# A graph network on Trainium2: residual, norm and tables of the last layer as one stage by blocks

## The chip, the cores and the metric

One core of a Trainium2 chip runs the whole kernel as one program. The metric is the time on the device in microseconds (us), lower is better. A measurement of this kernel scatters by some 0.1% (6551.42 to 6558.74 us in three runs).

## The reference

A graph of 6250 nodes with 128 features each and 100,000 edges goes through two blocks, each with a residual:

```python
h = jnp.maximum(_layernorm(x, axis=-1), 0.0)
x = x + _L0_gnn_ref(h, edge_index, ...)
h = jnp.maximum(_layernorm(x, axis=-1), 0.0)
x = x + _L1_gnn_ref(h, edge_index, ...)
```

The first block, `_L0_gnn_ref`, is two layers of graph attention with three heads (GATv2). Each is followed by a dense layer over the nodes and a batch norm (mean and variance of each feature over all nodes) with a Relu:

```python
x_in = _gatv2(x, edge_index, Wl1, bl1, Wr1, br1, att1, bc1)
h = jax.nn.relu(_batchnorm(x_in @ W1 + b1, g1, be1))
h2 = _gatv2(h, edge_index, Wl2, bl2, Wr2, br2, att2, bc2)
out = jnp.concatenate([h2, x_in], axis=1) @ W2 + b2
return jax.nn.relu(_batchnorm(out, g2, be2))
```

The second block, `_L1_gnn_ref`, makes a query from one end of each edge and a key and a value from the other (`embeds @ qTrans`, `kTrans`, `vTrans`), weighs the values by a clipped exponential per head, sums them for each node, adds `embeds`, and ends with a layer norm that has a scale and a bias:

```python
out = (res - mu) * jax.lax.rsqrt(var + 1e-06) * ln_scale + ln_bias
```

## The kernel before

The nodes are padded to 49 blocks of 128. An array of all nodes by 128 features is one tile of 128 x 6272 float32 (49 blocks side by side). `k.y2` and `k.hT` are two such tiles. `k.hT`, and `k.y2` up to the residual, hold a feature in each partition (a column is a node). From the residual on `k.y2` holds a node in each partition (a block's 128 columns are its features). Both lie in the tile `feat_area`, with a work area behind them; `node_area` holds other arrays by node.

The program is a series of stages. Each is a `nc.Block()`: every engine runs its own function, semaphores inside it set the order of the work, and a stage begins on every engine only when all engines have ended the one before it. `k.recycle()` is a small stage of its own in which SyncE clears, one after the other, all semaphores that were taken since the last recycle. `pipeline(...)` writes a loop over the blocks, unrolled by two, in which every engine goes round a ring of two buffers.

The stages that matter here, in order:

- **First layer's end.** `batch_norm` (tag "1", L1702) finds scale and shift of the batch norm from `k.hT`. `relu_in_place` (L1758) applies them and the Relu to all of `k.hT` by one ScalarE instruction (L1765). `k.recycle()` follows.
- **Tables of the second GATv2 layer.** `node_tables`, by `table_parts` (L1105): for each block ScalarE takes the features into a stage buffer (`take`, L1167), TensorE multiplies them by two weight matrices (L1157, L1158), ScalarE copies one product to a buffer (`copy`, L1173) from which SyncE stores it to DRAM (L1143), and VectorE keeps the other in SBUF. Take and copy go round two buffers each, and a copy waits until the store from its buffer has landed.
- **The edges, the dense layer** and `batch_norm` (tag "2") on `k.y2`.
- **Residual**, `residual_rows` (L1772): SyncE loads x (3.2 MB) into the place of `k.hT` (L1008, L1010); VectorE waits for all of it. For each block ScalarE applies scale, shift and Relu (L1788), TensorE turns the block so that a partition is a node (L1799), and VectorE adds x to it and writes it back to `k.y2` (L1811). Then `k.recycle()`.
- **Norm**, `norm_to_features` (L1095) by `norm_parts` (L1038) and `center` (L1013): VectorE and ScalarE go over the whole 128 x 6272 array one instruction at a time (sum L1018, subtract the mean L1020, square L1052, sum L1022, scale L1030); then for each block Relu on ScalarE (L1060), a transpose on TensorE (L1069) and a copy on VectorE into `k.hT` (L1083); at the end VectorE applies the Relu to the rows (L1086).
- **Tables of the attention**, `node_tables` again with other weights: key and value together (256 columns, L1157) go to DRAM, the query (128 columns, L1158) stays (`keep`, L1197).
- **Edges of the attention**, `edge_attention`; its first row on SyncE's queue is L1863.
- **The end**, `finish` (L1985): VectorE divides (L2036 to L2038), adds the features (L2041), takes mean and variance of each block (`bn_stats` L2043, `bn_aggr` L2046), ScalarE scales each block (L2027), VectorE multiplies by `ln_scale` and adds the residual (L2058, L2059) and SyncE stores. Beside this GpSimd adds `ln_bias` to the whole residual `k.y2` by one instruction (L2019).

## Time and profile before

| | |
|---|---|
| Time, median of 3 runs | 6554.96 us (6551.42 to 6558.74) |
| The profiled execution's own time | 6546.25 us, 8.71 us below that median |
| Its span, first to last instruction | 6544.4 us |
| Busy: PE, DVE, ACT, POOL | 76%, 85%, 66%, 61% of the span |
| Mean granted TensorE clock | 0.91 of 2.4 GHz |
| Residual to the last table, 5193.05 to 5367.15 us | 174.10 us |
| First layer's Relu, L1765 | 5.61 us |
| The end, from 6476.2 us | 68 us |

PE is TensorE, DVE VectorE, ACT ScalarE, POOL GpSimd, SP SyncE; a q behind a name is the engine's sequencer, which issues its instructions and DMAs. A clock of 1.00 is 2.4 GHz, of 0.50 it is 1.2 GHz. Where stages follow each other with a barrier, the time of the whole is the sum of the stages, and within a stage the loop's slowest chain sets the time, not the busiest engine's share. The idle time in brackets behind a row of the timeline is that of the row's engine before it, with what ended it.

### The profile page before, as it was taken

The page shows a single profiled execution, that of the slowest core. Times are in us where ns is not written, and L with a number is a line of the kernel's source. Part 1 is how long each engine was busy: PE and PEld are TensorE (multiplying, and loading weights), DVE is VectorE, ACT ScalarE, POOL GpSimd, SP SyncE. Part 2 cuts the span into 40 slices and gives each one's busy share as a digit, 9 for nine tenths or more (in the row PEclk, how much of TensorE's full clock was granted, in tenths as well). Part 3 has the DMA queues.
Part 4 walks back from the last instruction along what each step waited for, and adds up shares of the span by engine and source line. Part 5 has one row for each costly group of instructions (what it writes and reads, how often), then busy time and mean ns, then how long its engine had stood idle before and what let it go on. Part 6 is the DMA issues. An engine that isn't in the chain of part 4 may idle for free. (4 is left out here: it accounts for less than half of the span.)

```text
span 6544.4 us, 130007 instructions
## 1 busy us (share of the span) xinstructions
PE 4986.5 (76%) x23046; PEld 2906.8 (44%) x23047; DVE 5557.6 (85%) x13086; ACT 4324.9 (66%) x19265; POOL 3959.7 (61%) x3547
## 2 busy tenths in 40 slices
PE   3796899842888889888878899889998645555663
PEld 2573455421444444444463444444444435555552
DVE  9999988732999999999857999999999547777777
ACT  5576799720899999999837999999999430000001
POOL 0588877785666666666405666666665017777774
PEclk9999999966999999999989999999999767777776
DMA  0362000132555555555515555555556024444444
GB/s 13 62 81 22 2 2 2 11 53 52 146 139 139 140 139 139 140 139 140 100 41 144 140 140 140 139 141 141 139 139 128 23 67 127 127 126 126 126 126 73
DMA packets 397652, 656.25 MB, mean 100 GB/s; under 512 B 141767, under 2 KB 259461, under 8 KB 397044
## 3 DMA queue, kind: packets, MB, share of 16 engines
q0 software_dynamic: 185888, 481.62, 29.0%
q1 hardware_dynamic: 211540, 172.59, 11.3%
q14 instruction: 199, 1.63, 0.1%
q8 instruction: 25, 0.41, 0.0%
HBM read 617.73 MB, written 33.88 MB: 100 GB/s over the span
## 5 line engine op out<-in xcount | busy, mean ns | idle before, releaser
L1272 POOL DMA_INDIRECT feat_area<-xl_table,feat_area x1856 | 2007.0, 1081 | 1476.7 <-PE bank L1346 668.4
L1423 ACT ACTIVATE feat_area<-feat_area 128x130 f32<-128x130 f32 x5568 | 1643.5, 297 | 237.2 <-DVE feat_area L1476 234.0
L1333 PE MATMUL bank<-node_area,feat_area 128*128 x3712 | 1472.3, 520 | 339.4 <-DVE feat_area L1468 174.4
L1407 ACT ACTIVATE feat_area<-feat_area 128x128 f32<-128x128 f32 x4640 | 1442.1, 387 | 30.7 <-issue 30.7
L1346 PE MATMUL bank<-feat_area 128*128 128x390 f32 x3712 | 1408.9, 502 | 33.7 <-ACT feat_area L1407 12.6
L634 POOL DMA_INDIRECT rec_by_dst<-feat_area,gather_col x800 | 1051.2, 1314 | 243.7 <-issue 233.1
L1856 POOL DMA_INDIRECT feat_area<-kv_table,feat_area x832 | 829.4, 997 | 562.3 <-DMA feat_area<-gather_src 309.0
L1333 PEld LDWEIGHTS bank<-node_area,feat_area 128*128 128x128 f32 x3712 | 634.7, 190 | 988.8 <-issue 731.1
L1423 ACT ACTIVATION_READ_ACCUMULATOR feat_area<-feat_area 128x1 f32 x5568 | 1040.2, 187 | 0.0
L1346 PEld LDWEIGHTS bank<-feat_area 128*128 128x128 f32 x3712 | 670.2, 190 | 601.6 <-issue 196.0
L1468 DVE TENSOR_TENSOR feat_area<-bank,feat_area 128x780 f32<-128x780 f32 x928 | 889.6, 959 | 24.4 <-DMA feat_area<-xl_table,feat_area 17.8
L1476 DVE SCALAR_TENSOR_TENSOR feat_area<-feat_area 128x780 f32<-128x780 f32 x928 | 889.6, 959 | 0.0
L1911 ACT ACTIVATE feat_area<-feat_area 128x32 f32<-128x32 f32 x208 | 47.7, 230 | 1052.7 <-DVE feat_area L1952 1052.7
L1898 PE MATMUL bank<-feat_area 128*128 128x136 f32 x1664 | 357.6, 378 | 448.3 <-DVE feat_area L1963 448.1
L835 PE MATMUL bank<-feat_area 125*128 125x416 f16 x3200 | 571.4, 340 | 8.5 <-ACT feat_area L856 8.5
L856 ACT ACTIVATE feat_area<-feat_area 125x128 f16<-125x128 f16 x1600 | 514.2, 391 | 70.4 <-DVE feat_area L793 50.4
L1898 PEld LDWEIGHTS bank<-feat_area 128*128 128x128 f32 x1664 | 302.1, 264 | 497.8 <-DVE node_area L1978 341.6
L1515 DVE SCALAR_TENSOR_TENSOR node_area<-node_area,stays,bank 128x390 f32 x812 | 497.0, 612 | 16.9 <-PE bank L1346 16.7
L835 PEld LDWEIGHTS bank<-feat_area 125*128 125x128 f16 x3200 | 312.5, 98 | 267.4 <-DVE feat_area L795 9.1
L795 DVE TENSOR_SCALAR feat_area<-feat_area 125x832 f16<-125x832 f16 x800 | 408.1, 510 | 0.0
L1001 DVE TENSOR_TENSOR feat_area<-iota_f,lo_col 128x256 f32<-128x256 f32 x928 | 382.9, 413 | 0.0
L1939 DVE TENSOR_TENSOR feat_area<-feat_area,bank 128x512 f32<-128x512 f32 x208 | 143.0, 688 | 260.4 <-DMA feat_area<-kv_table,feat_area 259.3
(320 smaller groups left out, 6823.2 us busy)
## 6 DMA issues: line engine op xcount, KB each, us to landing
feat_area<-lo_slot SPq DMA_DIRECT2D x464, 128.0 KB, 3.3
feat_area<-xl_table,feat_area POOLq DMA_INDIRECT x1856, 3.4
feat_area<-lo_slot_src SPq DMA_DIRECT2D x208, 128.0 KB, 3.3
node_area<-lo_edge SPq DMA_DIRECT2D x100, 256.0 KB
xl_table<-feat_area SPq DMA_DIRECT2D x98, 195.0 KB, 3.3
feat_area<-kv_table,feat_area POOLq DMA_INDIRECT x832, 3.0
rec_by_dst<-feat_area,gather_col POOLq DMA_INDIRECT x800
feat_area<-gates SPq DMA_DIRECT2D x348, 32.0 KB
```

The costliest lines, as they stand in the source:

```text
L634: pool.indirect_dma_start(k.rec_d, bass.IndirectOffsetOnAxis(ap=self.pos[:, c:c + 1], axis=0), self.pay[:, c, :], None).then_inc(self.writ ...
L835: last = nc.tensor.matmul(out[n][m], self.to_lane[s][:, n * P:(n + 1) * P], self.to_tile[s][:, m * half:(m + 1) * half], start=False, stop ...
L856: last = nc.scalar.activation(self.to_lane[s][:, n * P:(n + 1) * P], self.at_lane[s], ACT.Copy, scale=self.piece[n][:, ds(c, 1)])
L1272: pool.indirect_dma_start(ring[:, at:at + HE], None, k.xl, bass.IndirectOffsetOnAxis(ap=index[s // CG][:, n:n + 1], axis=0)).then_inc(gath ...
L1333: last = nc.tensor.matmul(pair[s % 2][:, u, 0:HE], pick[s // 2 % 2][:, c:c + P], k.node[:, ds(columns[0], HE)], start=True, stop=True)
L1346: last = nc.tensor.matmul(sums_in[s % 2], place[s % 2][:, u * P:(u + 1) * P], ring[:, at:at + HE], start=u == 0, stop=u == GS - 1)
L1407: last = nc.scalar.activation(row[:, 0:D], row[:, 0:D], ACT.Copy, scale=row[:, D:D + 1])
L1423: last = nc.scalar.activation(at, at, ACT.Copy, accum_out=score[s // CG][:, to:to + 1])
L1468: nc.vector.tensor_tensor(z[s % V].rearrange("p (u e) -> p u e", u=GS), pair[s % 2][:, :, 0:HE], ring[:, s * W:(s + 1) * W].rearrange("p ( ...
L1476: nc.vector.scalar_tensor_tensor(out=zu, in0=zu, scalar=0.0, in1=att_w.unsqueeze(1).to_broadcast([P, GS, HE]), op0=ALU.max, op1=ALU.mult). ...
L1856: pool.indirect_dma_start(kv[s][:, u * KV:(u + 1) * KV], None, k.kv, bass.IndirectOffsetOnAxis(ap=index[s][:, u:u + 1], axis=0)).then_inc( ...
L1898: last = nc.tensor.matmul(total[s % 2][u], place[s % 2][:, u * P:(u + 1) * P], wv[s % 2][:, u * VW:(u + 1) * VW], start=True, stop=True)
```

## The change

- `relu_in_place` is gone. `table_parts` takes a scale and a shift, and in the second layer's tables ScalarE's `take` is a Relu with this scale and shift in place of the copy.
- The load of x begins in the second `batch_norm`, behind its two small loads.
- `residual_rows`, the recycle behind it, `norm_to_features` and the tables of the attention are one stage, `residual_tables`, written out without loops, in two phases over the blocks. In the first, with rings of four, ScalarE applies scale, shift and Relu, TensorE turns the block, VectorE adds x, and takes mean and variance of each row by `bn_stats` and `bn_aggr`. Then the scale and offset of all blocks are found at once. In the second, ScalarE writes the normed rows with Relu to `h` (scale and offset are columns), TensorE turns them, VectorE copies them to `k.hT` and adds `ln_bias` to the block of `k.y2`, and two blocks behind TensorE makes the products, three behind ScalarE copies them out to a ring of four. The recycle stands behind this stage.
- `finish` no longer loads `ln_bias`, and GpSimd has no work in it.

Core of the diff:

```diff
@@ table_parts, take @@
-            nc.scalar.copy(stage[s], k.hT[:, ds((2 * j + s) * P, P)]).then_inc(staged[s], 1)
+            rows = k.hT[:, ds((2 * j + s) * P, P)]
+            if relu is None:
+                nc.scalar.copy(stage[s], rows).then_inc(staged[s], 1)
+            else:
+                nc.scalar.activation(stage[s], rows, ACT.Relu, bias=relu[1], scale=relu[0]).then_inc(staged[s], 1)
@@ batch_norm @@
             load_cols(nc, sp, cols, (gamma, beta), loaded)
+            if early is not None:
+                x, area, x_cleared, x_loaded = early
+                sp.wait_ge(x_cleared, 1)
+                load_nodes(sp, x, area, x_loaded)
...
             do = Order(dve, order)
+            if early is not None:
+                x, area, x_cleared, x_loaded = early
+                nc.vector.memset(area[:, (NB - 1) * D:NB * D], 0.0).then_inc(x_cleared, 1)
@@ residual_tables @@
+    w = cut(KV + D)
+    stage = [cut(P) for _ in range(4)]
+    out = [cut(KV) for _ in range(4)]
...
+        def _(sp):
+            for c, v in ((0, io["L1_gnn_kTrans"]), (D, io["L1_gnn_vTrans"]), (KV, io["L1_gnn_qTrans"])):
+                sp.dma_start(w[:, c:c + D], v).then_inc(weights, 16)
+            sp.dma_start(last_bias, io["L1_gnn_ln_bias"].partition_broadcast(P)).then_inc(bias_ready, 16)
+            for b in range(NB):
+                sp.wait_ge(copied, b + 1)
+                sp.dma_start(k.kv[b * P:(b + 1) * P, :], out[b % 4]).then_inc(stored[b % 4], 16)
+            for s in range(4):
+                sp.wait_ge(stored[s], 16 * ((NB + 3 - s) // 4))
...
+        def _(act):
+            for b in range(NB):
+                if b >= 4:
+                    act.wait_ge(turned, b - 3)
+                nc.scalar.activation(stage[b % 4], k.y2[:, at(b)], ACT.Relu, bias=shift, scale=scale).then_inc(staged, 1)
+            act.wait_ge(var_set, 1)
+            nc.scalar.activation(rstd, rstd, ACT.Sqrt).then_inc(rooted, 1)
+            act.wait_ge(shifted, 1)
+            for t in range(NB + 3):
+                if t < NB:
+                    nc.scalar.activation(h[:, at(t)], k.y2[:, at(t)], ACT.Relu, bias=offset[:, t:t + 1],
+                                         scale=rstd[:, t:t + 1]).then_inc(normed, 1)
+                b = t - 3
+                if b >= 0:
+                    act.wait_ge(done, b + 1)
+                    if b >= 4:
+                        act.wait_ge(stored[b % 4], 16 * (b // 4))
+                    nc.scalar.copy(out[b % 4], k.bank[2 + b % 3][:, 0:KV]).then_inc(copied, 1)
...
+        def _(pe):
+            for b in range(NB):
+                pe.wait_ge(staged, b + 1)
+                if b >= 4:
+                    pe.wait_ge(kept, b - 3)
+                nc.tensor.transpose(k.bank[b % 4][:, 0:P], stage[b % 4], k.ident[:, :]).then_inc(turned, 1)
+            pe.wait_ge(weights, 48)
+            for t in range(NB + 2):
+                if t < NB:
+                    pe.wait_ge(normed, t + 1)
+                    if t >= 2:
+                        pe.wait_ge(moved, t - 1)
+                    nc.tensor.transpose(k.bank[t % 2][:, 0:P], h[:, at(t)], k.ident[:, :]).then_inc(flipped, 1)
+                b = t - 2
+                if b >= 0:
+                    pe.wait_ge(moved, b + 1)
+                    if b >= 3:
+                        pe.wait_ge(copied, b - 2)
+                        pe.wait_ge(q_kept, b - 2)
+                    nc.tensor.matmul(k.bank[2 + b % 3][:, 0:KV], k.hT[:, at(b)], w[:, 0:KV], start=True, stop=True)
+                    nc.tensor.matmul(k.bank[5 + b % 3][:, 0:D], k.hT[:, at(b)], w[:, KV:KV + D], start=True,
+                                     stop=True).then_inc(done, 1)
...
+        def _(dve):
+            do = Order(dve, order)
+            dve.wait_ge(x_loaded, 32)
+            for t in range(NB + 2):
+                if t < NB:
+                    dve.wait_ge(turned, t + 1)
+                    nc.vector.tensor_tensor(k.y2[:, at(t)], k.bank[t % 4][:, 0:P], k.hT[:, at(t)], ALU.add).then_inc(kept, 1)
+                if 0 <= t - 1 < NB:
+                    dve.wait_ge(kept, t)
+                    nc.vector.bn_stats(stats[:, 6 * (t - 1):6 * t], k.y2[:, at(t - 1)]).then_inc(measured, 1)
+                if 0 <= t - 2:
+                    dve.wait_ge(measured, t - 1)
+                    nc.vector.bn_aggr(agg[:, 2 * (t - 2):2 * (t - 1)], stats[:, 6 * (t - 2):6 * (t - 1)]).then_inc(merged, 1)
...
+            for t in range(NB + 1):
+                if t < NB:
+                    dve.wait_ge(flipped, t + 1)
+                    nc.vector.tensor_copy(k.hT[:, at(t)], k.bank[t % 2][:, 0:P]).then_inc(moved, 1)
+                    nc.vector.tensor_tensor(k.y2[:, at(t)], k.y2[:, at(t)], last_bias, ALU.add).then_inc(added, 1)
+                b = t - 1
+                if b >= 0:
+                    dve.wait_ge(done, b + 1)
+                    nc.vector.tensor_copy(q_area[:, at(b)], k.bank[5 + b % 3][:, 0:D]).then_inc(q_kept, 1)
@@ finish @@
-        @block.gpsimd
-        def _(pool):
-            pool.wait_ge(loaded, 32)
-            nc.gpsimd.tensor_tensor(x3, x3, bias.unsqueeze(1).to_broadcast([P, NB, D]), ALU.add).then_inc(offset, 1)
```

How the order of instructions changes, on VectorE (DVE) from the residual to the norm's scale. Before:

```order
L1811 TENSOR_TENSOR feat_area<-bank,feat_area 128x128
L1777 UNCONDITIONAL_BRANCH
L1102 UNCONDITIONAL_BRANCH
L1018 TENSOR_REDUCE feat_area<-feat_area 128x49
L1019 TENSOR_SCALAR feat_area<-feat_area 128x49
L1020 TENSOR_TENSOR node_area<-feat_area 128x6272
L1022 TENSOR_REDUCE feat_area<-node_area 128x49
L1023 TENSOR_SCALAR feat_area<-feat_area 128x49
L1025 RECIPROCAL feat_area<-feat_area 128x49
L1030 TENSOR_TENSOR node_area<-node_area,feat_area 128x6272
L1083 COPY feat_area<-bank 128x128 x2
```

With the change, at the start of phase 1:

```order
L1839 TENSOR_TENSOR feat_area<-bank,feat_area 128x128 x2
L1842 BN_STATS feat_area<-feat_area 128x6
L1839 TENSOR_TENSOR feat_area<-bank,feat_area 128x128
L1842 BN_STATS feat_area<-feat_area 128x6
L1845 BN_AGGR feat_area<-feat_area 128x2
L1839 TENSOR_TENSOR feat_area<-bank,feat_area 128x128
```

And at the step from phase 1 to phase 2:

```order
L1847 TENSOR_SCALAR feat_area<-feat_area 128x49
L1849 RECIPROCAL feat_area<-feat_area 128x49
L1850 SCALAR_TENSOR_TENSOR feat_area<-feat_area 128x49
L1856 COPY feat_area<-bank 128x128
L1857 TENSOR_TENSOR feat_area<-feat_area 128x128
L1856 COPY feat_area<-bank 128x128
L1857 TENSOR_TENSOR feat_area<-feat_area 128x128
L1861 COPY node_area<-bank 128x128
L1856 COPY feat_area<-bank 128x128
```

The four instructions over the whole 128 x 6272 array are gone (as are L1052 on ScalarE and L1086 behind the transposes); two short ones for each block, L1842 and L1845, find mean and variance. In phase 2 a block's L1856, L1857 and L1861 take the places of L1083, of the addition on GpSimd and of L1197.

On TensorE (PE), the transposes of the norm and the products of the tables. Before, the one loop behind the other:

```order
L1069 MATMUL bank<-ident,feat_area 128x128
L1098 UNCONDITIONAL_BRANCH
L1210 UNCONDITIONAL_BRANCH
L1157 MATMUL bank<-feat_area 128x256
L1158 MATMUL bank<-feat_area 128x128
L1157 MATMUL bank<-feat_area 128x256
L1158 MATMUL bank<-feat_area 128x128
```

With the change, in the second phase:

```order
L1821 MATMUL bank<-ident,node_area 128x128 x3
L1828 MATMUL bank<-feat_area 128x256
L1829 MATMUL bank<-feat_area 128x128
L1821 MATMUL bank<-ident,node_area 128x128
L1828 MATMUL bank<-feat_area 128x256
L1829 MATMUL bank<-feat_area 128x128
```

The transpose of a block (L1821) now stands directly ahead of the two products (L1828, L1829) of the block two before it.

## Rows read from the trace of the kernel before

**Rows 1.** Windows: busy time of each engine, granted clock and DMA, by stage.

```profile
core 0: us, PE busy (x) PEld busy (x) DVE busy (x) ACT busy (x) POOL busy (x), PEclk, DMA share, GB/s
5193.05:5240.60 47.55, 20.75 (x49) 8.94 (x49) 14.33 (x51) 21.55 (x49) 0.00 (x0) 0.50 0.24 67
5240.60:5304.40 63.80, 16.39 (x49) 8.98 (x49) 43.35 (x57) 18.55 (x51) 0.00 (x0) 0.50 0.00 0
5304.40:5367.15 62.75, 42.09 (x196) 34.07 (x196) 14.30 (x49) 30.32 (x98) 0.00 (x0) 0.93 0.31 106
```

**Rows 2.** Timeline: start, duration, engine, line, [idle before <-releaser]; the load of x and the residual.

```profile
5182.70 0.43 SPq L1603 DMA_DIRECT2D feat_area<-in_L_gnn_be  x1
...
5193.39 0.79 SPq L1008 DMA_DIRECT2D feat_area<-in_x  x1
...
5207.68 0.49 DVE L1811 TENSOR_TENSOR feat_area<-bank,feat_area 128x128 f32<-128x128 f32 x2 [14.39 <-DMA feat_area<-in_x]
...
5209.86 0.88 ACT L1788 ACTIVATE feat_area<-feat_area,bn_shift,bn_scale 128x128 f32 x2 [0.28 <-PE bank L1799]
...
5210.41 0.18 PEld L1799 LDWEIGHTS bank<-ident,feat_area 128*128 128x128 f32 x1 [0.59 <-ACT feat_area L1788]
...
5240.60 6.69 DVE L1018 TENSOR_REDUCE feat_area<-feat_area 128x49 f32<-128x6272 f32 x1 [5.05 <-PEq L206]
```

**Rows 3.** Timeline of the attention's tables: the loop at the lower clock, its stores, then later.

```profile
5308.66 1.06 PE L1157 MATMUL bank<-feat_area 128*128 128x256 f32 x2
...
5309.30 56.06 SPq L1143 DMA_DIRECT2D kv_table<-feat_area  x49
...
5309.94 1.06 PE L1157 MATMUL bank<-feat_area 128*128 128x256 f32 x2
...
5332.14 0.37 ACT L1173 COPY feat_area<-bank 128x256 f32<-128x256 f32 x1
...
5332.40 0.30 ACT L1167 COPY feat_area<-feat_area 128x128 f32 x1
...
5332.85 0.60 PE L1157 MATMUL bank<-feat_area 128*128 128x256 f32 x2
...
5333.64 0.37 ACT L1173 COPY feat_area<-bank 128x256 f32<-128x256 f32 x1 [0.94 <-DMA kv_table<-feat_area]
...
5333.83 0.29 DVE L1197 COPY node_area<-bank 128x128 f32 x1 [0.37 <-PE bank L1158]
...
5367.15 0.25 SPq L1863 DMA_DIRECT2D feat_area<-block_s  x1
```

**Rows 4.** Windows, columns as in rows 1: the same tables some 6 us after their first product.

```profile
5313.00:5316.00 3.00, 2.50 (x13) 1.92 (x11) 1.08 (x4) 1.70 (x6) 0.00 (x0) 0.93 0.37 128
```

**Rows 5.** Timeline of the end: the division, the GpSimd addition and the statistics of the last norm.

```profile
6479.51 6.69 DVE L2038 TENSOR_TENSOR node_area<-node_area,feat_area 128x6272 f32<-128x6272 f32 x1
6479.69 17.66 POOL L2019 TENSOR_TENSOR feat_area<-feat_area 128x6272 f32<-128x6272 f32 x1 [25.76 <-DMA feat_area<-in_L_gnn_ln_bias]
6486.23 17.66 DVE L2041 TENSOR_TENSOR node_area<-node_area 128x6272 f32<-128x6272 f32 x1
6503.93 9.57 DVE L2043 BATCH_NORM_STATS2 feat_area<-node_area 128x6 f32<-128x128 f32 x49
6513.53 3.33 DVE L2046 BATCH_NORM_AGGREGATE feat_area<-feat_area 128x2 f32<-128x6 f32 x49
6516.90 0.19 DVE L2048 TENSOR_SCALAR feat_area<-feat_area 128x49 f32<-128x49 f32 x1
...
6518.15 18.96 ACT L2027 ACTIVATE node_area<-node_area,feat_area 128x128 f32<-128x128 f32 x49 [0.78 <-DVE feat_area L2051]
```

**Rows 6.** Timeline of the first layer's Relu, and of the tables that follow it.

```profile
3369.69 5.61 ACT L1765 ACTIVATE feat_area<-feat_area,bn_shift,bn_scale 128x6272 f32<-128x6272 f32 x1 [1.29 <-PEq L1713]
...
3378.88 0.50 ACT L1167 COPY feat_area<-feat_area 128x128 f32<-128x128 f32 x2 [3.58 <-PEq L206]
...
3422.81 0.56 DVE L1195 TENSOR_TENSOR node_area<-bank,feat_area 128x390 f32 x1 [0.84 <-PE bank L1158]
...
3423.17 0.48 ACT L1173 COPY feat_area<-bank 128x390 f32<-128x390 f32 x1 [0.74 <-DMA xl_table<-feat_area]
```

More of the change, by code:

```diff
@@ L1092, in norm_parts, with table_parts @@
     return on_sync, on_scalar, on_tensor, on_vector, wait_features
[L1095 to L1102 removed]
 def by_head(v):
     return v.rearrange("p (h w) -> p h w", h=H)
[L1109 removed]
+def table_parts(k, gathered_w, local_ws, gather_w, local_w, table, local, bias_rows, att, tag, relu=None):
     nc = k.nc
@@ L1746, in layer_tables, with gat_layer @@
     return k, (w["Wl"],), (w["Wr"],), HE, HE, k.xl, k.node, (w["bl"], w["br"]), w["att"], f"{n}"
[L1749 removed]
+def gat_layer(k, io, n, relu=None):
     if n == 1:
```

86 lines of the change are left out of this document (28 added, 58 removed).

## The prediction

> **What bounds the kernel now.** I read the pages from the coarse to the fine: the times and the slices, the windows by stage, then the timeline inside each stage that the change touches. The two long edge stages and the sort are not touched, so everything is decided in three places where stages follow each other behind barriers. The largest is the stretch from the residual to the last table, 174.1 us in three stages [rows 1]: 47.6 for the residual, 63.8 for the norm, 62.8 for the tables. No engine is full in the first two: PE 20.75 of 47.55, VectorE 43.35 of 63.80. In the residual VectorE first waits 14.39 us for x, and a recycle costs 5.05 us at its end [rows 2]. In the norm whole-array instructions stand one behind the other. In the tables SyncE stores 49 blocks in 56.06 us, 1.14 us each, and ScalarE waits for a store to land before it copies into the same buffer, 0.94 us idle in the row shown [rows 3]. The second place is the end, where VectorE's addition L2041 takes 17.66 us and the division L2038, of the same size, 6.69 [rows 5]. The third is the first layer's Relu, 5.61 us in a stage of its own [rows 6].
>
> **The load of x.** From its issue at 5193.39 to VectorE's first addition at 5207.68 are 14.3 us [rows 2]. Now it stands behind the batch norm's small loads, of which the last is issued by 5183.1: x lands at 5183.2 + 14.3 = 5197.5. It still ends after the batch norm, whose successor begins at 5193.05 [rows 1], so 4 us of wait stay. The memset for it costs VectorE 0.2 us under this wait.
>
> **Phase 1.** VectorE has three short instructions per block. Two additions take 0.49 and a single short one 0.29 [rows 2, 3], so 0.20 apart; `bn_stats` is 9.57 / 49 = 0.195, `bn_aggr` 3.33 / 49 = 0.068 [rows 5]: 0.463 us a block. ScalarE needs 0.39 (two in 0.88, one 0.49 [rows 2]) and the ring of four takes the hand-over out of the chain, so VectorE sets the pace: 49 x 0.463 = 22.7, and 0.3 to drain, ends at 5220.5. The waits between the three might cost: upper bound 0.65 a block, the three single durations less overlap, +9 us; I take 0.463, since L2043 and L2046 also stand written out and run without gaps. From the variance to ScalarE's first scaled row are 1.25 us (6516.90 to 6518.15 [rows 5]): 5221.8.
>
> **Phase 2.** What a product costs at each clock: at the lower one a block's two products come 1.28 us apart (5308.66, 5309.94 [rows 3]) for 2 x (256 + 128) columns, 1.67 ns a column, so half of that at the higher one, 0.64 us; the transpose is one pass of 128 columns, 0.21 or 0.11. TensorE alone would need 1.49 or 0.75 us a block, ScalarE 0.39 + 0.26 = 0.65, VectorE 3 x 0.20 = 0.60. But the waits tie ScalarE and TensorE in a ring: ScalarE may copy block t-2 only when TensorE's turn t is done, and the relu of block t+2 stands behind that copy in its queue. Copy to relu 0.26 [rows 3]; relu to TensorE's weight load 0.55 (5209.86 to 5210.41 [rows 2]); weight load 0.09 (half of 0.18 [rows 2]) and transpose 0.11; products to their reader 0.98 (5332.85 to 5333.83 [rows 3]). Sum 1.99 us for two blocks, 1.0 each. Bounds: 0.75, TensorE alone (-11 us), and the pace that the stores had, 1.14 (+6). I take 1.0, since each link has a row. With four buffers a store may take four blocks' time, so its wait should go.
>
> The clock starts low. In the tables the first product came about 1.4 us before the second block's at 5308.66, and in the window from 5313 the clock is 0.93 [rows 3, 4]: some 6 us, in which 4 blocks pass at 1.5. So: 5221.8, a head of 1.9 (relu 0.55, transpose, second block, copy to `k.hT`, an estimate from the same rows), 4 x 1.5 = 6.0, 45 x 1.0 = 45, and a tail of 2.8 (0.98 - 0.64 = 0.34 until the last product can be read, copy 0.37, 0.3 to issue the last store, estimated from the small load's 0.43 [rows 2], and 5367.15 - 5365.36 = 1.8 from its issue's end to the next stage [rows 3]): 5277.5.
>
> **The recycle** moves behind this stage. It clears 73 semaphores in a gap of 5.05 us [rows 2] and 53 in one of 3.58 [rows 6], 0.074 each; now there are 89, 6.2 us, of which 0.5 for the change of stage is in the tail already. The edges then begin at 5283.2, not 5367.15: **84 us saved**.
>
> **The end.** GpSimd's addition and VectorE's L2041 both show 17.66 us. They fit one engine at a time: VectorE's L2038 until 6486.2, GpSimd until 6497.35, then VectorE for 6.5, which is what L2038 took [rows 5]. Without the GpSimd addition L2041 should take 6.69: **11.0 us saved**. The Trainium skill (SBUF — State Buffer, SBUF: two separate sides) says so too: an operation of VectorE with two inputs in SBUF and one of GpSimd that reads SBUF lock the shared port, and the later one waits entirely. If it were a share of bandwidth instead, the durations would not be equal and L2041 would gain about as much. The addition itself goes to VectorE in phase 2, where it has room (0.60 of 1.0).
>
> **The first layer.** The Relu's stage goes: 5.61 and about 0.5 for its barrier, 6.1 us. In the tables the take grows by 0.19 (0.49 against 0.30 [rows 2, 3]). The copy there waits for the store's landing at 3423.17, 0.36 after the product was done for VectorE at 3422.81 [rows 6], so 0.19 fits into the slack; if none did, 49 x 0.19 = 9.3. I take 1.0: **5.1 us saved**.
>
> **Sum.** 84 + 11.0 + 5.1 = 100 us of the profiled execution's 6546.25 us, 6446. That execution stood 8.7 us below the median of the runs shown, 6554.96, and I predict for the median: **6455 us**, 1.5% less.
>
> **Rivals.**
> - *The clock stays low in phase 2.* In the residual and the norm TensorE was busy up to 20.75 of 47.55 us with nothing but 98 transposes, and the clock stood at 0.50 [rows 1]. In the tables it rose, at products alone; here a transpose stands ahead of each pair. Against it: 1.28 of 1.49 us are products at the lower clock, 0.64 of 1.0 at the higher, no less than the tables' 0.64 of 1.14, which held. Price 45 x 0.5 = 22.5 us: 6477. Chance 0.12. The Trainium skill (TensorE: Matmul & The Clock Gate, Part 4: PE-mode transpose) says that transposes don't count as TensorE's activity; by that rule the low clock under transposes alone agrees with rows 1, and whether the mix rises is open.
> - *The stores stay the bound*, because the DMA queue's rate, not one store's latency, gives the 1.14: 45 x 0.14 = 6 us more, 6461. Against it: x came at 3.2 MB in 14.3 us, 0.6 us for a store's 131 KB. Chance 0.1.
> - *TensorE's own pace is reached* in phase 2, 0.75 to 0.85: 7 to 11 us less, 6446. Chance 0.1.
> - *L2041 stays at 17.66*, since it alone has both inputs in `node_area`: 6466. The equality of the two durations speaks against it. Chance 0.07. So the change wouldn't do what its last part says.
> - *Slower.* The waits make the new stage serial: each block goes through ScalarE, TensorE and VectorE before the next may start. Phase 1 would be 0.55 + 0.5 + 0.3 = 1.4 us a block, phase 2, at a clock that then stays low, 0.55 + 0.5 + 0.35 + 1.8 + 0.4 = 3.6. That is 49 x 5.0 = 245 against the 74 of my sum, +171 on -100: 6626. It decides from 3.5 us for a block's both phases. Against it: the order rows show rings of three and four and TensorE two blocks behind, and the old loops overlapped with rings of two. Chance 0.03, with it any stall of the long written-out code.
>
> **How the numbers follow.** The forecast with its bounds has 0.58. The cases between 6446 and 6477 and the forecast's own bounds, phase 1 at +9 and the takes at +8 among them, fill 6436 to 6481, which is the range. A difference of 0.2%, 13 us, is about what a measurement of this kernel can tell from no change. Faster by more than that in all cases but the last and what I have not thought of: 0.95; within it 0.02; slower 0.03.
>
> **What would show it.** In the new profile: the first addition of phase 1 near 5197.5 minus the 6 us from the first layer, 49 of them in 23 us; ScalarE's phase 2 at 1.0 us a block with TensorE waiting for ScalarE's relu, the clock 1.00 after some 6 us; no wait for stored rows; L2041's successor at 6.7 us; GpSimd with nothing at the end; the edge stage as long as before, 1109 us from 5367.15 to the end's start. Wrong if phase 2 runs at 1.5 with the clock at 0.50, if the copies wait for stores, or if the edges' stages change their length.

## The result, and the profile after

The changed kernel takes **6443.35 us**, the median of four runs (6437.28 to 6446.37), against 6553.64 us for the kernel before (four runs, 6551.42 to 6558.74). The ratio is 0.9836, with a 95% interval from 0.9824 to 0.9848: faster by 1.6%, 110 us. The range on record, 6436 to 6481, holds it; the 6455 forecast is 12 us high.

Between the two profiled executions, 6546.25 and 6444.68 us, are 101.6 us, where the sum forecast 100. The stretches, each from the first issue of its first stage to that of the next (the sort is taken with the first layer), were:

```
stretch                                   before     after    moved
start of the first batch norm            3358.97   3357.69     -1.3
first batch norm to second tables          19.89     13.78     -6.1
second layer's tables                      87.80     90.58     +2.8
second layer's edges                     1633.92   1637.56     +3.6
node stage after them                      81.75     81.88     +0.1
second batch norm to attention's edges    184.82     96.11    -88.7
attention's edges                        1109.08   1108.25     -0.8
the end                                    68.17     56.85    -11.3
```

Nearly all of it came from the residual, norm and tables, as forecast. The windows of the changed kernel over its two phases, from the first addition to the last copy (the columns are those of [rows 1]), and then four inside its second phase:

```profile
core 0: us, PE busy (x) PEld busy (x) DVE busy (x) ACT busy (x) POOL busy (x), PEclk, DMA share, GB/s
5197.49:5221.33 23.84, 19.78 (x45) 8.17 (x45) 23.42 (x150) 18.68 (x43) 0.00 (x0) 0.50 0.01 2
5221.33:5270.40 49.07, 45.63 (x245) 37.91 (x245) 33.74 (x147) 37.35 (x98) 0.00 (x0) 0.94 0.37 127
5223.00:5226.00 3.00, 3.00 (x11) 2.64 (x12) 1.10 (x6) 0.76 (x2) 0.00 (x0) 0.50 0.01 3
5226.00:5229.00 3.00, 2.91 (x14) 2.46 (x13) 1.90 (x9) 2.05 (x6) 0.00 (x0) 0.74 0.26 90
5229.00:5232.00 3.00, 2.91 (x19) 2.47 (x17) 2.13 (x10) 2.36 (x7) 0.00 (x0) 1.00 0.49 169
5232.00:5250.00 18.00, 17.11 (x100) 14.26 (x99) 13.28 (x59) 14.81 (x40) 0.00 (x0) 1.00 0.41 140
```

Where the three stages of before left every engine partly idle, phase 1 now has one that is nearly full: VectorE, 23.42 of 23.84 us, with the clock at 0.50. In phase 2 TensorE is the busiest, 45.63 of 49.07 us (the ends of its instructions are modelled, and the ring below shows that it still waits). The clock is at 0.50 in the first 3 us of the windows shown, then 0.74, then 1.00.

The timeline of the changed kernel around the load of x, where [rows 2] had an idle of 14.39 us:

```profile
5182.50 0.80 SPq L1008 DMA_DIRECT2D feat_area<-in_x  x1
...
5192.89 3.18 ACT L1793 ACTIVATE feat_area<-feat_area,bn_shift,bn_scale 128x128 f32<-128x128 f32 x8 [1.88 <-PEq L1707]
...
5197.49 0.49 DVE L1839 TENSOR_TENSOR feat_area<-bank,feat_area 128x128 f32<-128x128 f32 x2 [5.71 <-DMA feat_area<-in_x]
```

The load takes 15.0 us from its issue, where it took 14.3 before, and VectorE waits 5.71 us for it. That the batch norm beside it makes it longer is not shown: in `x_late` below, where it runs behind the batch norm again, it also takes 15.0.

The timeline of phase 2 in the changed kernel at full clock, one round of two blocks:

```profile
5249.85 0.37 ACT L1806 COPY feat_area<-bank 128x256 f32<-128x256 f32 x1 [0.32 <-PE bank L1829]
...
5250.12 0.49 ACT L1799 ACTIVATE node_area<-feat_area 128x128 f32<-128x128 f32 x1
...
5250.67 0.14 PEld L1821 LDWEIGHTS bank<-ident,node_area 128*128 128x128 f32 x1 [0.28 <-ACT node_area L1799]
...
5250.83 0.61 PE L1828 MATMUL bank<-feat_area 128*128 128x256 f32 x2
...
5251.70 0.37 ACT L1806 COPY feat_area<-bank 128x256 f32<-128x256 f32 x1 [0.32 <-PE bank L1829]
```

This is the ring that the prediction describes, link by link: copy to relu 0.27, relu to TensorE's weight load 0.55, to the products 0.16, products to their reader 0.87. Together they make 1.85 us, 5249.85 to 5251.70, for two blocks, 0.92 each. ScalarE waits for TensorE (0.32) and TensorE for ScalarE (0.28), so neither is full. The waits of phase 2, from 5222 to 5272, say the same (waiting side, side that it waits for, us in total, times, longest):

```profile
ACT feat_area L1806 <- PE bank L1829: 11.1, 27, 1.8
PEld bank L1821 <- ACT node_area L1799: 6.8, 23, 0.5
...
ACT feat_area L1806 <- DMA kv_table<-feat_area: 0.5, 1, 0.5
```

The copy waits for a store once in 49 blocks, where before it did so in the steady loop [rows 3].

The end, in the timeline of the changed kernel, answers to [rows 5]:

```profile
6389.13 6.69 DVE L2080 TENSOR_TENSOR node_area<-node_area,feat_area 128x6272 f32<-128x6272 f32 x1
6395.86 6.69 DVE L2083 TENSOR_TENSOR node_area<-node_area 128x6272 f32<-128x6272 f32 x1
```

The addition of `h` (now L2083) takes 6.69 us, as the division does, and GpSimd does nothing there.

### The profile page after: what moved, and what is told of

Read it like the earlier page. It is cut to its first block and busy times, and to the rows that moved or that the text cites. A ratio compares the mean times of both kernels' runs of the same rounds, so it can differ in the third digit from the quotient of the medians.

```text
span 6442.7 us, 128936 instructions
## 1 busy us (share of the span) xinstructions
PE 4969.3 (77%) x23046; PEld 2900.6 (45%) x23047; DVE 5533.3 (86%) x13228; ACT 4317.3 (67%) x19214; POOL 3919.0 (61%) x3546
## 5 line engine op out<-in xcount | busy, mean ns | idle before, releaser
L1266 POOL DMA_INDIRECT feat_area<-xl_table,feat_area x1856 | 1986.0, 1070 | 1497.4 <-PE bank L1340 688.2
```

Of the source, the lines that this page charges most:

```text
L1266: pool.indirect_dma_start(ring[:, at:at + HE], None, k.xl, bass.IndirectOffsetOnAxis(ap=index[s // CG][:, n:n + 1], axis=0)).then_inc(gath ...
```

## The experiments

Each kernel is the changed one with one edit. Two of the chips used run every kernel more slowly, the one before too (7579 to 7597 us instead of 6535 to 6554), in stages that no edit here touches; so of runs there only the stretches beside them and their instructions are compared, always with other runs on such a chip. Each experiment names the time of the kernel before. All kernels but the last two were run once, and stretches that an edit doesn't touch differ by some us (the first batch norm began between 3350.8 and 3356.7 us in four kernels on one chip). So what an edit does is read from its stretch and not from the whole time: `out_ring_two`, whose stretch is 13 us longer than that of `copy_four_behind`, ends only 2 us later.

### The last bias back at the end: `bias_at_end`

GpSimd adds the bias in the last stage again, and phase 2 doesn't.

```diff
-                    nc.vector.tensor_tensor(k.y2[:, at(t)], k.y2[:, at(t)], last_bias, ALU.add).then_inc(added, 1)
...
+        @block.gpsimd
+        def _(pool):
+            pool.wait_ge(loaded, 32)
+            part = x3[:, 0:49, :]
+            nc.gpsimd.tensor_tensor(part, part, bias.unsqueeze(1).to_broadcast([P, 49, D]), ALU.add).then_inc(offset, 1)
```

> The changed kernel with ln_bias added at the end again, by one GpSimd instruction over the whole residual, and no longer by VectorE in phase 2. One engine at a time: VectorE's addition of the features behind the division shows about 17.7 us again in place of 6.69, and the end grows by 11 us (from 56.9 us between the first instruction of the end and the last of the kernel to 68). Rival, the change of data or place of the arrays made that addition short: it stays at 6.7 us. In phase 2 VectorE has one instruction less per block; as ScalarE and TensorE set the pace there it stays at 0.92 us a block; if VectorE did, it falls by 0.2, 9 us in all.

It took 7490.81 us beside 7597.32 before. Its timeline at the end:

```profile
7424.16 6.69 DVE L2086 TENSOR_TENSOR node_area<-node_area,feat_area 128x6272 f32<-128x6272 f32 x1
7424.34 17.66 POOL L2067 TENSOR_TENSOR feat_area<-feat_area 128x6272 f32<-128x6272 f32 x1 [29.48 <-DMA feat_area<-in_L_gnn_ln_bias]
7430.89 17.66 DVE L2089 TENSOR_TENSOR node_area<-node_area 128x6272 f32<-128x6272 f32 x1
```

The two durations of 17.66 us are back, so the GpSimd addition is what made L2041 long in the kernel before: 11 us. The end as a whole took 67.8 us, against 56.8 in `relu_whole` and `x_late` on the same chip. The other half is that VectorE's addition in phase 2 costs nothing that shows: without it the first relu to the last copy took 48.6 us (5929.0 to 5977.6), with it 48.7 in the changed kernel's profile (5221.33 to 5269.99) and 47.8 in another run of it.

### Half of it: `bias_half_at_end`

The same, but GpSimd adds to blocks 0 to 24 and VectorE, in phase 2, to 25 to 48.

```diff
-                    nc.vector.tensor_tensor(k.y2[:, at(t)], k.y2[:, at(t)], last_bias, ALU.add).then_inc(added, 1)
+                    if t >= 25:
+                        nc.vector.tensor_tensor(k.y2[:, at(t)], k.y2[:, at(t)], last_bias, ALU.add).then_inc(added, 1)
...
+            part = x3[:, 0:25, :]
```

> As bias_at_end, but GpSimd adds the bias of blocks 0 to 24 only, VectorE that of the others in phase 2. One engine at a time: GpSimd's own work is 25/49 of 11.1 us, 5.7 us, so it shows about 12.2 us (6.5 of waiting for the division ahead) and VectorE's addition behind it about 12.3 (5.7 of waiting and 6.6 of its own). Rival, both run together and each is slowed while the other runs: the addition is slowed only for the part that overlaps, so it shows about 6.7 + 5.7/2, 9.5 us, and GpSimd overlaps with the division too, which then is longer than 6.69.

It took 7467.81 us (before 7597.32). Its timeline at the end:

```profile
7406.61 6.69 DVE L2088 TENSOR_TENSOR node_area<-node_area,feat_area 128x6272 f32<-128x6272 f32 x1
7406.73 12.28 POOL L2069 TENSOR_TENSOR feat_area<-feat_area 128x3200 f32<-128x3200 f32 x1 [32.80 <-DMA feat_area<-in_L_gnn_ln_bias]
7413.33 12.22 DVE L2091 TENSOR_TENSOR node_area<-node_area 128x6272 f32<-128x6272 f32 x1
```

This tells taking turns from sharing. In turns, the division runs its full 6.69 until about 7413.3; GpSimd then does its whole work until 7406.73 + 12.28 = 7419.01; VectorE follows with 6.5 us until 7425.55. That gives 5.7 us for GpSimd's own work on 25 blocks, and 49/25 of it is 11.2, while the full case gave 17.66 - 6.5 = 11.1. Sharing would have made the division longer and the last addition 9.5 us. The division is untouched at 6.69, and the addition took 12.22: the engines take turns on whole instructions. The Trainium skill (SBUF — State Buffer, SBUF: two separate sides), which says that they lock a shared port, holds here in both sizes.

### The Relu back in a stage: `relu_whole`

```diff
+        relu_in_place(k, scale[:, 0:1], shift[:, 0:1], "1")
-        gat_layer(k, io, 2, (scale[:, 0:1], shift[:, 0:1]))
+        gat_layer(k, io, 2)
```

`relu_in_place` is the one ACTIVATE of before over 128x6272, in a block of its own.

> The changed kernel with the first layer's Relu as one instruction in a stage of its own again, and copies in the takes. By my working the stage costs 6.1 us and the longer takes 1.0. The traces of before and after show 6.1 and 2.8 (tables stage 87.8 and 90.6 us). If the takes are the cause the tables stage is back at 87.8 within 0.5; if the 2.8 us are scatter of the stores, it stays near 90.6 or falls elsewhere. Net against the changed kernel: 3.3 us longer by the traces, 5.1 by my working.

It took 7476.06 us (before 7597.32). From the first batch norm to the second layer's tables it took 19.9 us (4038.3 to 4058.2), 6.1 more than the 13.8 of the changed kernel. The tables themselves took 87.1 us (4058.2 to 4145.3). With the takes doing the Relu, the same stage on such chips took 88.2, 89.0 and 88.6 us in the three kernels beside it, and 90.2 in another run. So the takes cost 1 to 3 us, and the part nets 3 to 5 us: the sign is as forecast, the size not well told, since the stage itself scatters by 2 us. The waits of TensorE and of the copy over the whole stage (with the Relu in the takes, in all eight such runs, it took 88.2 to 90.6 us) say a little of where the cost goes. First the kernel before, from 3379 to 3466:

```profile
ACT feat_area L1173 <- DMA xl_table<-feat_area: 34.6, 46, 1.5
...
PE bank L1157 <- ACT feat_area L1167: 0.4, 2, 0.2
```

and then the changed kernel, from 3372 to 3462:

```profile
ACT feat_area L1167 <- DMA xl_table<-feat_area: 29.1, 41, 1.8
...
PE bank L1147 <- ACT feat_area L1161: 1.9, 7, 0.5
```

The longer take eats 5.5 us of the copy's wait for its store, as intended. TensorE's products now stand still for the take 1.9 us in 7 turns where it was 0.4 in 2; in `relu_whole`, without the longer take, it is 0.2 once. The weight loads waited for the take before as well (20.3 us in 43 turns, now 22.3 in 42), so take, product and copy were a ring with two buffers already. That the 1.5 us more are the longer take going round this ring fits, but no run separates it from the scatter of the stage.

### x loaded where it was: `x_late`

```diff
-        batch_norm(k, k.y2, g["g2"], g["be2"], scale[:, :], shift[:, :], "2", (io["x"], k.hT, x_cleared, x_loaded))
+        batch_norm(k, k.y2, g["g2"], g["be2"], scale[:, :], shift[:, :], "2")
...
+            sp.wait_ge(x_cleared, 1)
+            load_nodes(sp, io["x"], k.hT, x_loaded)
```

> The changed kernel with the load of x issued at the start of the new stage, as before. x takes 14.3 us from its issue, and the first addition then waits about 14.4 us in place of 5.7: the stage is 9 to 10 us longer (my working had 10.3 earlier, 4 of wait left). If something else held the first addition (the first transposes, the barrier), it is less than 5 us longer.

It took 7477.33 us (before 7597.32). Its timeline at the start of the new stage:

```profile
5888.20 0.79 SPq L1008 DMA_DIRECT2D feat_area<-in_x  x1
...
5903.23 0.49 DVE L1842 TENSOR_TENSOR feat_area<-bank,feat_area 128x128 f32<-128x128 f32 x2 [15.12 <-DMA feat_area<-in_x]
```

The stretch from the batch norm to the edges took 105.3 us (5877.1 to 5982.4), against 95.9 and 95.8 in `bias_at_end` and `relu_whole` on the same chip (94.5 in `bias_half_at_end`) and 95.4 in another run of the changed kernel: the early load is worth 9.4 to 9.9 us, 10.8 by the shortest of them. VectorE's wait, 15.12 instead of 5.71, makes 9.4 of it.

### One more block of lag in phase 2: `copy_four_behind`

ScalarE copies block t-4 at turn t instead of t-3, which opens the ring.

```diff
-            for t in range(NB + 3):
+            for t in range(NB + 4):
...
-                b = t - 3
+                b = t - 4
```

> The changed kernel with ScalarE's copy to the store buffer four blocks behind its relu, not three. My theory: phase 2 goes at 0.92 us a block because two turns of TensorE are tied to one ring (copy, relu, transpose, products, 1.85 us). With the copy one block later three turns share the ring, 0.62 each, and TensorE alone is the bound: 0.75 to 0.78 us a block, 6 to 8 us less. Rival: TensorE or the stores already set the pace (its matrix products show 17.1 of 18 us busy): 0.92 as it is.

It took 6434.18 us (before, on that chip, 6535.26). Its windows in the steady stretch of phase 2, and the waits of the phase:

```profile
5226.00:5244.00 18.00, 18.00 (x108) 16.16 (x108) 14.62 (x66) 15.99 (x44) 0.00 (x0) 1.00 0.45 157
```

```profile
ACT feat_area L1806 <- PE bank L1829: 7.1, 25, 1.4
...
PEld bank L1821 <- ACT node_area L1799: 0.5, 1, 0.5
```

TensorE's wait for the relu is gone (0.5 us once, where the changed kernel has 6.8). First relu to last copy took 44.7 us, where it was 48.7 in the changed kernel's profile and 47.8 in `tables_ring_four` on the same chip (5199.68 to 5247.53): 3.1 to 4.0 less, where 6 to 8 were expected. So the ring was the bound, and what stands behind it is nearer than 0.75 us a block: two blocks take 1.69 us, 0.845 each.

It is tempting to call this TensorE's own pace, since the window shows it busy for all of the 18 us. The timeline speaks against it:

```profile
5240.18 0.29 DVE L1861 COPY node_area<-bank 128x128 f32<-128x128 f32 x1 [0.24 <-PE bank L1829]
...
5240.39 0.28 DVE L1856 COPY feat_area<-bank 128x128 f32<-128x128 f32 x1
...
5240.79 0.14 PEld L1821 LDWEIGHTS bank<-ident,node_area 128*128 128x128 f32 x1
...
5240.95 0.66 PE L1828 MATMUL bank<-feat_area 128*128 128x256 f32 x2
...
5241.56 0.14 PEld L1821 LDWEIGHTS bank<-ident,node_area 128*128 128x128 f32 x1
...
5241.87 0.29 DVE L1861 COPY node_area<-bank 128x128 f32<-128x128 f32 x1 [0.24 <-PE bank L1829]
```

Every second transpose comes late, and its weight load starts 0.12 us after the end of VectorE's copy L1856 of the block two before, for which it waits (`moved`), since the transposes have two banks. The same 0.12 stands at the start of phase 2 in the changed kernel (L1856 ends at 5222.81, the load starts at 5222.93), where the profile names L1856 as what the transpose waited for. That copy stands on VectorE behind L1861, which waits for the products. So there is a second ring, over VectorE and TensorE: L1861 to L1856 0.21, to the weight load 0.40, to the products 0.16, to L1861 0.92, together 1.69 us for two blocks. The turn that nothing holds takes 0.77 (5240.79 to 5241.56), close to the 0.75 of the prediction. This ring is read from the trace; no kernel opens it.

### Two buffers for the rows to store: `out_ring_two`

```diff
-    out = [cut(KV) for _ in range(4)]
+    out = [cut(KV) for _ in range(2)]
...
-                    if b >= 4:
-                        act.wait_ge(stored[b % 4], 16 * (b // 4))
+                    if b >= 2:
+                        act.wait_ge(stored[b % 2], 16 * (b // 2))
```

> The changed kernel with two store buffers in the new stage, as the old tables had, not four. If the old pace of 1.14 us a block was the latency of a store that two buffers wait for, phase 2 goes back to 1.1 to 1.2 us a block, 9 to 12 us more, with ScalarE's copies waiting for stores. If four buffers made no difference and the written-out code or the removed takes did, it stays at 0.92.

It took 6436.43 us (before 6535.26). First relu to last copy took 57.7 us, 9.0 more than the changed kernel's profile and 9.9 more than `tables_ring_four` on the same chip. The copy's wait for stores in phase 2 is this:

```profile
ACT feat_area L1806 <- DMA kv_table<-feat_area: 17.5, 35, 1.3
```

That is about 1.1 us a block, the 1.14 that the stage had before [rows 3]. The DMA view of the same kernel from 5235 to 5240 gives the stores' time from issue to landing (its last line: issues, KB each, median us):

```profile
kv_table<-feat_area SPq DMA_DIRECT2D x4, 128.0 KB, 1.7
```

So the pace of the old tables comes back with two buffers, each waiting for its store to land, and it is not the rate of the queue: with four buffers the stores go at 0.92 us a block in the changed kernel and at 0.845 in `copy_four_behind`, and the copy waits for a store once in each.

### The same in the second layer's tables: `tables_ring_four`

The tables with the Relu take get four buffers and banks instead of two, and the take runs two blocks ahead.

```diff
+    R = 2 if relu is None else 4
-    stage = [cut(P) for _ in range(2)]
-    out = [cut(gather_w) for _ in range(2)]
+    stage = [cut(P) for _ in range(R)]
+    out = [cut(gather_w) for _ in range(R)]
...
-        pipeline(act, NB, [(1, take), (0, copy)])
+        pipeline(act, NB, [(1 if R == 2 else 2, take), (0, copy)], R)
```

> The changed kernel with rings of four (take, product, copy, store) in the tables of the second GATv2 layer. If the longer take costs there because take, product and copy share a ring of two with a store's landing, the pace falls to TensorE's own, four passes of 390 columns, 1.31 us a block against 1.43, and the stage from 90.6 to 85 us. If the stores' rate is the bound (195 KB each), it stays at 1.4 us a block.

It took 6421.0 us (before 6535.26). The tables took 81.1 us (3366.0 to 3447.1), against 88.2 to 88.6 in the three kernels beside it: 7.1 to 7.5 less. Expected were 85 us, 5.6 less than the 90.6 of the profile, and the pace of 1.31 us a block came as expected (copies at 3409.86 and 3411.17). Its window, and its waits there:

```profile
3380.00:3440.00 60.00, 60.00 (x181) 34.54 (x181) 25.35 (x45) 39.67 (x90) 0.00 (x0) 0.98 0.40 147
```

```profile
ACT feat_area L1168 <- PE bank L1149: 32.6, 45, 12.7
```

TensorE is full (58.17 of 60 us in the changed kernel) and no wait for a store or a take is left. This takes back both the takes' cost and the stores' wait that was there before the change; as all rings grew together, it doesn't tell how much each was.

### Products among the transposes of phase 1: `products_in_phase_one`

From block 24 on, a product of the staged block, which nobody reads, goes ahead of each transpose of phase 1. Would the clock then be up when phase 2 begins?

```diff
+                if b >= 24:
+                    nc.tensor.matmul(k.bank[7][:, 0:P], stage[b % 4], k.ones[:, :], start=True, stop=True)
```

> The changed kernel with one more product per block ahead of the transpose in phase 1, from block 24 on; its result is read by nobody. TensorE has room there. If the granted clock rises under products and not under transposes, the windows show 0.50 while only transposes run, and 1.00 before phase 2 begins, whose first blocks then take 0.92 and not 1.5 us (2 us less in phase 2; phase 1 may lose as much while TensorE needs 0.85 us a block at the lower clock). If it rises with how busy TensorE is, it must have risen in phase 1 without them, or stays low with them too.

It took 6429.2 us (before 6535.26). Its windows through phase 1 and into phase 2:

```profile
5185.00:5196.00 11.00, 10.18 (x27) 5.22 (x28) 10.78 (x70) 9.33 (x21) 0.00 (x0) 0.50 0.01 3
5196.00:5199.00 3.00, 3.00 (x23) 3.00 (x22) 2.94 (x20) 2.59 (x7) 0.00 (x0) 0.77 0.00 0
5199.00:5202.00 3.00, 3.00 (x23) 2.42 (x22) 3.00 (x22) 3.00 (x9) 0.00 (x0) 1.00 0.02 5
...
5205.00:5208.00 3.00, 1.16 (x9) 0.73 (x7) 2.96 (x21) 0.00 (x0) 0.00 (x0) 1.00 0.00 0
5208.00:5210.00 2.00, 0.14 (x1) 0.14 (x1) 0.85 (x3) 1.02 (x3) 0.00 (x0) 1.00 0.00 0
5210.00:5213.00 3.00, 2.77 (x10) 2.14 (x10) 1.58 (x7) 1.64 (x5) 0.00 (x0) 0.67 0.00 0
```

With transposes nearly alone (the first product stands at 5194.46) TensorE is busy 10.18 of 11 us and the clock is at 0.50, the 1.2 GHz level. With products between the transposes it goes to 0.77 and then 1.00, the 2.4 GHz level, in phase 1 already. The first half agrees with the Trainium skill (TensorE: Matmul & The Clock Gate, Part 4: PE-mode transpose), that transposes don't count as activity; the second answers what the prediction left open, whether a mix of both rises. The edit brought nothing, though. TensorE had nothing to do for 3.7 us between the last transpose of phase 1 and the first of phase 2, at 5209.86. The clock was still 1.00 there and fell in the window from 5210, to 0.67 in the mean of 3 us, when the first products of phase 2 ran. Phase 2 took 47.8 us, as in `tables_ring_four` on the same chip, and the whole stretch 95.0, against 95.4 and 96.1 in two runs of the changed kernel.

### Four edits together, beside the changed kernel: `all_four` and `changed_again`

`all_four` has `copy_four_behind` and `tables_ring_four`; the clears of a recycle spread over four engines' queues; and x loaded one stage earlier still, in the node stage ahead of the batch norm.

```diff
-                for s in self.passing:
+                for s in self.passing[0::4]:
...
+            @block.scalar
+            def _(act):
+                for s in self.passing[1::4]:
+                    act.sem_clear(s)
...
-        batch_norm(k, k.y2, g["g2"], g["be2"], scale[:, :], shift[:, :], "2", (io["x"], k.hT, x_cleared, x_loaded))
+        node_layer(k, (g["bl2"], g["bc2"]), (g["W2"][0:HD, :],), ((k.y2, None, True),), "2",
+                   (io["x"], k.hT, x_cleared, x_loaded))
```

> The changed kernel with four more edits: the copy four blocks behind, rings of four in the second layer's tables, each recycle's clears split over SyncE, ScalarE, TensorE and VectorE, and the load of x issued at the start of the second dense layer, some 80 us earlier. From the single runs: 4 us from the copies and 7 from the rings. From my 0.074 us a semaphore: the first layer's recycle goes from 52 in a row to 13, 2.9 us less; the last from 89 to 25 (99 in all with the larger rings), 4.7 less. If a recycle's time is its barriers and not the clears, these two fall by less than 1 us. x has landed before phase 1: its wait of 5.7 us goes; the rival, that the reads of x slow the dense layer or that phase 1 then waits for its first transposes, gives 3 or less. Sum about 24 us less than the changed kernel, 0.4%.

> The changed kernel itself, unedited, on the same chip as all_four, as its yardstick: as measured, 0.98 of the kernel before. The tables of the second layer took 90.6 us in its profile and 88.2 to 88.6 in three others with the same tables: 88.4 here if that was one slow store, 90.6 if it belongs to this kernel.

Both ran on the same slower chip, beside nine runs of the kernel before at 7578.66 us. `changed_again`, the changed kernel unaltered, took 7472.17 us (four runs, 7461.68 to 7482.26), a ratio of 0.9858 (0.9841 to 0.9875). `all_four` took 7449.76 us (five runs, 7435.21 to 7472.59), 0.9831 (0.9811 to 0.985). The medians are 22.4 us apart, where about 24 were expected; the two intervals overlap, so by the whole time alone this is not sharp, but the stretches of the two profiles place 20.6 us of it:

```
stretch                                changed_again  all_four   moved
first batch norm to second tables               13.8      12.6    -1.2
second layer's tables                           90.2      80.3    -9.9
second batch norm to attention's edges          95.4      85.9    -9.5
```

The 90.2 us of `changed_again` answer its other question: the 90.6 of the first profile were not one slow store, but with 88.2 to 89.0 in six other kernels they don't belong to the changed kernel as such either.

In the last stretch, phase 1's first addition came 11.9 us after the batch norm's first issue instead of 16.1, 4.3 less. The wait for x is gone, and what stands there instead is the wait for TensorE in the timeline of `all_four`:

```profile
5878.14 0.60 DVE L1862 TENSOR_TENSOR feat_area<-bank,feat_area 128x128 f32<-128x128 f32 x2 [1.64 <-PE bank L1837]
```

Phase 2 took 44.2 us instead of 47.8. The recycle moved least: in the timelines of the two kernels, ScalarE's idle time ahead of the edges. The changed kernel run again:

```profile
5981.61 1.28 ACT L1959 ACT_TABLE_LOAD   x1 [7.24 <-PEq L206]
```

and `all_four`:

```profile
5952.13 1.28 ACT L1982 ACT_TABLE_LOAD   x1 [5.43 <-PEq L206]
```

That is 1.8 us less and 1.2 us at the first batch norm, where 4.7 and 2.9 had been expected of taking three quarters of the clears off one queue. The clears themselves stand in the traces (count, shortest, median and longest duration in ns, first and last start). On SyncE in `changed_again`, and on TensorE in `all_four`, both in the last recycle:

```profile
L210 SPq EVENT_SEMAPHORE_RANGE_CLEAR  x89: 25/25/30, 5976.5 to 5981.3; - x89
```

```profile
L220 PEldq EVENT_SEMAPHORE_RANGE_CLEAR  x25: 56/56/56, 5948.9 to 5951.8; - x25
```

SyncE's 89 clears take 4.8 us, 0.055 each and not 0.074. TensorE's 25 take 2.9, 0.12 each, while SyncE is through with its 25 in 1.3 (5948.8 to 5950.1), ScalarE in 1.6 and VectorE with 24 in 1.9. The recycle ends with the slowest queue: 4.8 - 2.9 = 1.9 us less, and 1.8 were measured. In the first recycle SyncE's 52 take 2.8 and TensorE's 13 take 1.5: 1.3 less, with 1.2 measured. An even split over four queues was the wrong one.

## Why the prediction was right

**The load of x.** Forecast for the first addition 5197.5; it came at 5197.49. That it fits to 0.01 us is luck: the load took 15.0 us instead of 14.3, and the batch norm began 0.8 us earlier and not the 6 us that the signs of the prediction subtract, as the tables (+2.8) and stretches that the change doesn't touch took most of the first layer's gain back. From the start of the new stage at 5192.89 the wait is 4.6 us, where the text said 4; the 5.71 of the row count from VectorE's last instruction in the batch norm. `x_late` shows that this part is worth 9.4 us or somewhat more.

**Phase 1.** Forecast 0.463 us a block from three instructions that the trace of before showed only apart. From the first addition to the end of the last `bn_aggr`, 5220.05, are 22.56 us, 0.460 a block, where 22.7 and 0.3 to drain were forecast. The upper bound, 0.65, was not needed: hand-overs between VectorE's instructions cost nothing here, where two others stand between them. Variance to the first relu: 1.25, as forecast.

**Phase 2.** The mechanism was right: the ring over ScalarE and TensorE sets the pace, and `copy_four_behind` shows it by opening it. The size was off by 0.07 a block, 1.85 us for two where the links summed to 1.99. Most of it is in one term, "products to their reader 0.98", which was taken from the old tables; here it is 0.87, and why it was longer there is open. The other links measured 0.27, 0.55 and 0.16 where 0.26, 0.55 and 0.20 stood. As 0.92 against the 1.0 of the sum this is 3.6 us of gain over 45 blocks. "TensorE alone 0.75", the lower bound, was near: a turn of TensorE that nothing holds takes 0.77. What stands behind the ring was missed, though: a second one over VectorE and TensorE at 0.845, so that opening the first doesn't reach TensorE's own pace.

**The clock.** Forecast some 6 us and four slow blocks; it was 4 us and three (first products at 5223.20, 5224.70, 5226.19, 1.49 apart as forecast). From the first product to the last copy are 46.8 us where the forecast's terms have 6 + 45 + 0.34 = 51.3; beside the 3.6 of the ring that leaves 0.9 for the clock. That transposes stand among the products did not matter, and the rival with the clock at 0.50, 6477 us, fell.

**The stores.** The wait went, as forecast, and the rival by which the queue's rate gives the 1.14 fell with `out_ring_two`: two buffers 1.1 a block, four 0.92.

**The recycle.** The edges began 6.9 us after the last store's issue, where tail and recycle together had 7.5. The total was near. The price of 0.074 per clear was too high: it came from two gaps, and the traces show 0.055 from clear to clear on SyncE, 4.8 us for the 89, and other prices on other queues (`all_four`).

**The end.** Forecast -11.0, measured -11.3, and taking turns is shown by two sizes. The rival by which L2041 stays at 17.66 fell.

**The first layer.** The stage that went was worth 6.1 us, as forecast. The takes were forecast at +1.0 and the profile has +2.8; by other runs it is 1 to 3. "0.19 fits into the slack" is the step that was weak: it looked at the copy's slack and not at TensorE, whose products stood still for the take 1.5 us longer than before.

**The sum.** Stretch by stretch the forecast has -84, -11.0 and -5.1, the profiles -88.7, -11.3 and -3.3, with +1.6 of scatter in stretches that the change doesn't touch. So that the sum came within 2 us of the 101.6 is partly luck: 4.7 too little in the large stretch, 1.8 too much in the first layer and 1.6 of scatter cancel. **The step that put the median too high**, by 10 of the 12 us, is the last one: the profiled execution before lay 8.7 us below its median, that of the changed kernel 1.3 above its own, and the forecast carried the first distance over. It is luck which execution is profiled; a saving by profile is good to such a distance and no better. The measured 6443 also lies below every case that the prediction priced (the lowest, TensorE's own pace, is 6446, or 6444 with its full 11 us); the lower end of the range, 6436, is not worked out in it.

The slower rival, a serial stage at 5.0 us a block for both phases, is refuted by the windows: both phases took 48.7 + 23.8 = 72.5 us in all, 1.5 a block.

## What to carry to other kernels

Before stages are merged, write down the ring of hand-overs through the engines for one turn with a row for each link, and divide by the blocks in flight; it gave the pace within 9%, where TensorE's busy sum, 0.75 against 0.92, was 18% low, and it says which lag to raise (one more block here took 3 to 4 us, two more buffers 9 to 10). When a ring is opened, write down the next one before calling an engine the bound: a window that shows TensorE busy for 18 of 18 us hid a wait in every second turn. When two long instructions on VectorE and GpSimd show the same duration in one stretch, test whether they take turns before counting either as its own cost. A load that is issued one stage ahead is paid only by what sticks out behind that stage, and when it no longer sticks out, the next thing in line takes over a part of the gain.

## What the runs showed of the hardware that was not expected

The changed kernel takes 6443 us on one chip and 7472 on another, 16% more. The work of ScalarE, VectorE and TensorE is as long on both (phase 2: 48.7 and 47.8 us). Between the two profiled executions 661 us of the difference lie ahead of the first layer's edges (which begin at 2288.3 instead of 1626.9) and 325 in attention's edges, while the second layer's edges took only 1656.5 instead of 1637.6. Attention's edges, first in the changed kernel's profile on the quicker kind:

```profile
5300.00:6380.00 1080.00, 637.60 (x3260) 586.28 (x3261) 783.65 (x2055) 47.27 (x206) 814.44 (x818) 0.73 0.48 124
```

and then `changed_again` on the slower:

```profile
6000.00:7415.00 1415.00, 639.19 (x3288) 572.31 (x3288) 776.86 (x2073) 47.84 (x208) 804.25 (x821) 0.68 0.37 95
```

Every engine has the same busy time within 2.4%, and the same bytes take longer, at 95 GB/s instead of 124. That the loads are what is slower is not shown: x, 3.2 MB, lands in 15.0 us on both kinds. So here savings in us could be compared between the chips and ratios could not: 101 to 110 us and 1.5 to 1.6% on the one, 106 us and 1.4% on the other.

Clearing a semaphore costs each queue another time: from start to start 0.055 us on SyncE, 0.066 on ScalarE, 0.084 on VectorE and 0.12 on TensorE (`all_four`).

TensorE's turn of a transpose and two products takes 1.49 us at the lower clock and 0.77 at the higher, in a turn that nothing holds: nearly half.
